# A graph and expert network on one core: where the two routers' logits are computed

## The reference, cut to what matters

```python
def _L0_ffn_ref(x, Wr, ...):            # x: layer norm of the sum, [6250, 256]
    rw = jax.nn.softmax(x @ Wr, axis=-1)            # Wr: [256, 8]
    topw, topi = jax.lax.top_k(rw, K)               # K = 2
    topw = topw / jnp.sum(topw, axis=-1, keepdims=True)
    ...
def _L1_ffn_ref(x, ..., gW, gb):
    gates = jax.nn.softmax(x @ gW + gb, axis=-1)    # gW: [256, 4], gb: [4]
    topv, topi = jax.lax.top_k(gates, TOPK)         # TOPK = 2
    topw = jax.nn.softmax(topv, axis=-1)
    ...
x = x + _L0_gnn_ref(_layernorm(x), ...)
x = x + _L0_ffn_ref(_layernorm(x), ...)
x = x + _L1_gnn_ref(_layernorm(x), ...)
x = x + _L1_ffn_ref(_layernorm(x), ...)
```

## Time and profile before

| | us |
|---|---|
| median of 3 runs | 6690.58 |
| lowest and highest | 6688.31, 6698.25 |
| the profiled execution's own time | 6698.42 |
| its span, first to last instruction | 6696.8 |
| TensorE busy | 4284.9 |
| VectorE busy | 3318.1 |
| GpSimd busy | 3481.7 |
| ScalarE busy | 827.6 |

### The profile page before, as it was taken

One profiled execution on the slowest core, in us unless ns is written; L12 is line 12 of the kernel. 1 busy time (PEld: TensorE's weight loads), 2 busy tenths in 40 slices (PEclk: granted clock), 3 DMA queues, 4 the chain that ended last, 5 costly groups with the idle time before them and its releaser, 6 DMA issues. The chain is left out here.

```text
span 6696.8 us, 90430 instructions
## 1 busy us (share of the span) xinstructions
PE 4284.9 (64%) x16771; PEld 3118.6 (47%) x16772; DVE 3318.1 (50%) x7834; ACT 827.6 (12%) x2019; POOL 3481.7 (52%) x3600
## 2 busy tenths in 40 slices
PE   1455566635666764556665379999971556667679
PEld 1333444423444443334443168888860344445435
DVE  6366666556566665656666521111126444444545
ACT  0200000020000002000000223322220000001322
POOL 3577777567777747777773060000016777774000
PEclk9777788867777887778887589999985778888789
DMA  5443333243333334333333241222225333333011
GB/s 184 126 111 106 106 106 106 71 140 106 106 106 106 106 90 121 106 106 106 106 106 89 77 132 38 64 64 51 65 67 152 105 105 105 105 105 97 1 46 44
DMA packets 485970, 642.49 MB, mean 96 GB/s; under 512 B 243204, under 2 KB 366208, under 8 KB 484096
## 3 DMA queue, kind: packets, MB, share of 16 engines
q0 software_dynamic: 175472, 478.82, 25.6%
q1 hardware_dynamic: 300880, 155.42, 8.3%
q10 hardware_dynamic: 9552, 7.61, 0.4%
HBM read 544.09 MB, written 97.86 MB: 96 GB/s over the span
## 5 line engine op out<-in xcount | busy, mean ns | idle before, releaser
L942 POOL DMA_INDIRECT rows<-table,ix x2352 | 2264.3, 963 | 741.5 <-issue 686.7
L1203 PE MATMUL acc<-rows,hot 128*128 x5856 | 1623.1, 435 | 227.2 <-DVE hot L1050 170.0
L1203 PEld LDWEIGHTS acc<-rows,hot 128*128 128x128 f32 x5856 | 1165.6, 212 | 640.9 <-issue 425.5
L1050 DVE TENSOR_TENSOR hot<-lanes,drel 128x256 f32<-128x256 f32 x1464 | 609.6, 422 | 580.0 <-PE acc L1203 577.3
L1249 POOL DMA_INDIRECT rows<-emb,ix x784 | 743.3, 948 | 261.2 <-issue 231.3
L1371 PE MATMUL acc<-rows,hot 128*128 x1952 | 571.1, 454 | 331.3 <-DVE hot L1292 312.3
L1044 DVE TENSOR_TENSOR rows<-rows,pw 128x1024 f32<-128x1024 f32 x588 | 711.2, 1210 | 0.0
L1371 PEld LDWEIGHTS acc<-rows,hot 128*128 128x128 f32 x1952 | 421.5, 228 | 463.7 <-issue 391.9
L1929 PE MATMUL p<-xt,w 128*128 128x256 f32 x2496 | 553.2, 380 | 26.1 <-DVE xt L1976 26.1
L1940 PE MATMUL p<-w,xT 128*128 128x256 f32 x2496 | 551.4, 379 | 0.0
L1929 PEld LDWEIGHTS p<-xt,w 128*128 128x128 f32 x2496 | 475.4, 190 | 91.0 <-issue 26.2
(11 more groups left out here) (394 smaller groups left out, 4166.2 us busy)
## 6 DMA issues: line engine op xcount, KB each, us to landing
rows<-table,ix POOLq DMA_INDIRECT x2352, 2.8
xg<-slots_in SPq DMA_DIRECT2D x632, 32.0 KB
slots_out<-ys SPq DMA_DIRECT2D x78, 256.0 KB
table<-hs SPq DMA_DIRECT2D x147, 130.0 KB, 2.0
own_row<-table SPq DMA_DIRECT2D x21, 896.0 KB, 11.3
slots_in<-zsp SPq DMA_DIRECT2D x9, 1664.0 KB, 22.2
xin<-in_x POOLq DMA_DIRECT2D x14, 896.0 KB, 5.6
rows<-emb,ix POOLq DMA_INDIRECT x784, 2.7
```

The lines of the kernel that those rows point to most:

```text
L942: pool.indirect_dma_start(rows[:, h * GB + k, 0:RW], None, table, bass.IndirectOffsetOnAxis(ap=ix[:, h, k:k + 1], axis=0)).then_inc(landed ...
L1050: v.tensor_tensor(hot[j][:, :, :], lanes[:, :, :].to_broadcast([P, 2, P]), c.drel[:, ds(q * W + j * 2, 2)].rearrange("p (k o) -> p k o", o ...
L1203: ins = nc.tensor.matmul(A, hot[j][:, k, :], four[:, j * 2 + k, :], start=False, stop=False, skip_group_check=True)
```

## The change

The routers no longer have a loop on TensorE and VectorE. `norm_stage` takes a pair (router weights, PSUM tile). With it, TensorE's list is written out for all 49 tiles: after the transposes of tile t come the two matmuls of tile t-1, which have the turned tile in `xT` as the stationary operand (128 x 128) and the router's weights (128 x E) as the moving one. Their result has the nodes on the partitions and goes to one PSUM tile `pG` of 49 x E columns, which fits in one bank and stays allocated until the router has read it. The router begins with one VectorE operation over all 49 tiles, a copy in router 1 and an addition of the bias in router 2; for this the bias is loaded onto all partitions. The load of `wr` moves ahead of norm 1. The semaphores of each router go from eight to three.

```diff
-def norm_stage(nc, kit, c, a, X, add, outs, want):
+def norm_stage(nc, kit, c, a, X, add, outs, want, route=None):
...
+                    if route is not None:
+                        wr, logits = route
+                        for t in range(NT + 1):
+                            if t < NT:
+                                pe.wait_ge(normed, t + 1)
+                                pe.wait_ge(kept, t // UT * UT + ring2(t % UT))
+                                for h in range(2):
+                                    ins = nc.tensor.transpose(pT[t % UT % 2][:, h, :],
+                                                              xs[:, t % UT, h * P:(h + 1) * P], c.ident[:, :])
+                                ins.then_inc(turned, 1)
+                            if t:
+                                m = t - 1
+                                pe.wait_ge(kept, UT + m + 1)
+                                for h in range(2):
+                                    nc.tensor.matmul(logits[:, m, :], outs["sbuf"][:, h, m * P:(m + 1) * P], wr[:, h, :],
+                                                     start=(h == 0), stop=(h == 1))
+                        return
...
-def router(nc, kit, c, xT, wr, E, gbias, at_f, w1, w2, gate):
+def router(nc, kit, c, pG, E, gbias, at_f, w1, w2, gate):
...
-        lt = sb("lt", [E, UT * P])
...
-        pL = [ps(f"pL{k}", [E, CH]) for k in range(2)]
-        pG = ps("pG", [P, UT, E])
-        prod, kept, turned, put, own = sem("prod"), sem("kept"), sem("turned"), sem("put"), sem("own")
-        asked, given, passed = sem("asked"), sem("given"), sem("passed")
+        own, asked, given = sem("own"), sem("asked"), sem("given")
         with nc.Block() as block:
-            @block.tensor
-            def _(pe):
-                with pe.Fori(0, NB) as i:
-                    pe.wait_ge(kept, i + 1)
-                    for m in range(2):
-                        for k in range(2):
-                            ins = nc.tensor.matmul(pL[m][:, :], wr[:, k, :], xT[:, k, ds(i * UT * P + m * CH, CH)],
-                                                   start=(k == 0), stop=(k == 1))
-                    ins.then_inc(prod, 1)
-                    pe.wait_ge(kept, i + 2)
-                    pe.wait_ge(put, i + 1)
-                    pe.sem_inc(passed, 1)
-                    for k in range(UT):
-                        ins = nc.tensor.transpose(pG[:, k, :], lt[:, k * P:(k + 1) * P], c.ident[0:E, 0:E])
-                    ins.then_inc(turned, 1)
...
-                for s in (kept, put, turned):
-                    dve.sem_inc(s, 1)
-                with dve.Fori(0, NB) as i:
-                    dve.wait_ge(prod, i + 1)
-                    dve.wait_ge(turned, i + 1)
-                    for m in range(2):
-                        to = lt[:, m * CH:(m + 1) * CH]
-                        if gbias is None:
-                            ins = v.tensor_copy(to, pL[m][:, :])
-                        else:
-                            ins = v.tensor_scalar(to, pL[m][:, :], gbias[:, :], None, ALU.add)
-                    ins.then_inc(kept, 1)
-                    dve.wait_ge(turned, i + 2)
-                    v.tensor_copy(logits[:, ds(i * UT, UT), 0:E], pG[:, :, :]).then_inc(put, 1)
                 ch = Chain(dve, own)
                 ch.n = 1
-                dve.wait_ge(put, NB + 1)
+                if gbias is None:
+                    ch.link(v.tensor_copy(logits[:, :, 0:E], pG[:, :, :]))
+                else:
+                    ch.link(v.tensor_tensor(logits[:, :, 0:E], pG[:, :, :], gbias[:, :, :].to_broadcast([P, NT, E]),
+                                            ALU.add))
...
-                    norm_stage(nc, kit, c, a, X, "input", {"sbuf": xT, "rows": slots_in, "rows_sb": rows}, "both")
                     loads(nc, kit, [(wr[:, :, :], a["L0_ffn_Wr"].rearrange("(k p) e -> p k e", p=P))])
-                    router(nc, kit, c, xT, wr, E0, None, pick, w1, w2, None)
+                    with kit.stage() as route:
+                        pG = route.ps("pG", [P, NT, E0])
+                        norm_stage(nc, kit, c, a, X, "input", {"sbuf": xT, "rows": slots_in, "rows_sb": rows}, "both",
+                                   (wr, pG))
+                        router(nc, kit, c, pG, E0, None, pick, w1, w2, None)
...
-                    (gb[:, :], a["L1_ffn_gb"])])
+                    (gb[:, 0, :], a["L1_ffn_gb"].rearrange("e o -> o e").to_broadcast([P, E1]))])
...
-                norm_stage(nc, kit, c, a, X, "scaled", {"sbuf": xT, "adds": rows, "scale": sumsq}, "turned")
-            with kit.stage() as st:
-                router(nc, kit, c, xT, gw, E1, gb, st.sb("pick", [P, NT, 2]), st.sb("w1", [P, NT, 1]),
-                       st.sb("w2", [P, NT, 1]), gate)
+                with kit.stage() as route:
+                    pG = route.ps("pG", [P, NT, E1])
+                    norm_stage(nc, kit, c, a, X, "scaled", {"sbuf": xT, "adds": rows, "scale": sumsq}, "turned",
+                               (gw, pG))
+                    router(nc, kit, c, pG, E1, gb, route.sb("pick", [P, NT, 2]), route.sb("w1", [P, NT, 1]),
+                           route.sb("w2", [P, NT, 1]), gate)
```

More of the change, by code:

```diff
@@ L2330, in program @@
             gate = rest.sb("gate", [P, NT, E1])
-            gw, gb = rest.sb("gw", [P, 2, E1]), rest.sb("gb", [E1, 1])
+            gw, gb = rest.sb("gw", [P, 2, E1]), rest.sb("gb", [P, 1, E1])
             with kit.stage() as st:
```

## The result

The changed kernel takes 6611.5 us (median of 4 runs, 6608.4 to 6615.5) against 6691.3 us for the kernel before: ratio 0.988, interval 0.9863 to 0.9897, 1.2% faster. The forecast was 6608 us. The profiled execution took 6608.4 us.

A forecast was written before the change was run, and what follows sets the result against it. No engine is full; serial stages bound it, the router loops being TensorE-VectorE chains. 90.5 - 5.6 - 2.9 + 0.8 = 82.8 us off 6698.42 gives 6615.6; median 7.8 lower, 6608 us; range 6598 to 6632.

The forecast's parts named there:

- router 1, memset to `max`: Router 1: 41.91 us shrink to 1.1, memset 0.39, PSUM copy 0.53 and waits some 0.1; 40.8 us saved.
- periods of full groups: Both norms: groups still follow each other at 11.01 and 10.12 us, the round of VectorE and ScalarE; cost 0.
- tail of norm 2: Last group of norm 2: 56 TensorE instructions, 12.3 us, end at 6344.3 instead of 6338.70; 5.6 us lost.
- tail of norm 1: Last group of norm 1: ScalarE's copy of the rows starts at 3805.0 instead of 3802.16, the last store 2.9 us later.
- load of `wr` moved: The `loads` stage goes ahead of norm 1, serial in either place: cost 0, bounds minus and plus 3.35 us.
- load of `gb`: The bias broadcast stands among loads that are broadcast already: cost 0, at most its own issue of 0.4 us.
- What bounds the kernel: Engines meet at each stage's end, so each us taken from or added to a stage moves the program's end as much.
- The price of a logit instruction: TensorE in the norms: 0.217 us per instruction, the weight load's spacing at any clock; four per tile, 0.87 us.
- The cover: Norms: TensorE's 9.1 us per group fit under periods of 10.12 and 11.01 us, so full groups cost nothing.
- the first rival: Norms: waits between transposes and logits leave holes, TensorE becomes the bound; 22 us more, 6630 us; chance 0.13.
- Loads that don't overlap: Norms: weight load and matmul run one behind the other, a tile takes 4.1 us; 6860 us; chance 0.03.
- Code fetching: TensorE's straight lists in the norms: a dozen more fetches at 1 to 3 us exposed, 6615 to 6640 us; chance 0.05.

The follow-up runs named there:

- the run with only the second half changed: Only norm 2, router 2 and the bias load changed against the kernel before: 6649.2 us, ratio 0.9935, 44.3 us less.
- The run with only the first half changed: Only norm 1 and router 1 changed against the kernel before: 6657.6 us, ratio 0.9947, 35.9 us less.
- The undisturbed burst: Changed kernel with all logits of each norm made in one burst behind its last transposes: 6683.8 us, ratio 0.9995 to the kernel before.
- the 64-column run: Changed kernel with two more matmuls per tile behind the logits, same stationary tile, 64 moving columns: 6661.3 us, ratio 0.9960 to the kernel before.

## Why the prediction was right

| step | predicted, us | measured in the profiles, us |
|---|---|---|
| router 1, memset to `max` | -40.8 | 41.91 to 1.02: -40.9 |
| router 2, memset to `max` | -49.7 | 50.60 to 0.82: -49.8 |
| fewer semaphores | -0.4 each | boundary behind router 1 from 1.38 to 1.03: -0.35 |
| periods of full groups | 0 | 11.00 and 10.12, unchanged |
| tail of norm 2 | +5.6 | first row of the stage to router 2's memset, 76.4 to 81.3: +4.8 |
| tail of norm 1 | +2.9 | first row to the landing of the last store: +2.5 |
| load of `wr` moved | 0 | ahead +2.4, behind -3.2: -0.8 |
| load of `gb` | 0, at most 0.4 | issue to the addition behind it, 3.64 to 4.34: +0.7 |
| sum | -82.8 | -84.0 |

(The measured sum takes the routers up to the next stage, 41.2 and 50.1.) The timed difference is 79.8 us, and its interval, 69 to 92 us, holds both sums. The profiled pair differs by 90.0 us; the 6 us beyond the table lie in stages that the change doesn't touch, nearly all ahead of norm 1, and the other profiles show that they move by chance.

That the forecast of 6608 us came within 4 us of the median is partly luck. Router 1's 40.8 us rest on one execution in which the old loop was slow; at the 38.27 us of the run with only the second half changed, the table's sum would be 80.4, next to the timed 79.8. That this is the typical value isn't shown: only these two profiles hold that loop. The run with only the first half changed fits it too: 35.9 us where 39.4 were expected. Small slips cancel or are too small to matter: 0.39 + 0.53 + 0.1 is 1.0 and not 1.1, and 3805.0 is 2.8 us and not 2.9 behind 3802.16.

**What bounds the kernel.** Right: the saving in each stage went through to the end unchanged. The stages between the routers took the same: from the first expert's weight load to the next weights' load 1246.7 us in both kernels.

**The price of a logit instruction.** Right as to clock and columns, a little high as a size. The undisturbed burst gives 0.213 us against the 0.217 read off and the earlier trace rows, and the 64-column run shows that the moving columns don't set it. That leaves the weight load or a fixed price per instruction. The old routers' small transposes, whose stationary operand has 8 rows instead of 128, speak against a fixed price: seven took 0.57 us together, less than 0.1 us apart. They are another kind of instruction, and no run changed the stationary operand alone. The Trainium skill ("TensorE: Matmul & The Clock Gate", section "LDWEIGHTS (loading the stationary operand)") gives a load the number of columns over 1.2 in ns, an estimate of 107 ns for 128 columns. That isn't what fp32 costs here: the measured 0.213 us is twice that. But a tile costs 1.17 us, not 1.30. Four logits instructions at 0.213 leave 0.32 for the two transposes, where a chain of transposes alone shows 0.43. The mix of transposes and logits is quicker than the two apart, which the prediction didn't count, and no run here says why. It explains norm 2's tail: 11.6 us from the last burst's release to the end instead of 12.3.

**The cover.** Right, and it is what the gain hangs on. Three runs show its edges: the same tile instead of the one before takes 65 us of the gain away, four more instructions per tile 52, all logits behind the norm 75 of 79, which leaves nothing that the times can tell. The holes of the first rival didn't come: in the steady stretch of the timeline transposes and logits follow each other without idle time. Besides the wait for the root, the one hole in a full group is the wait for tile 6's copy, 0.15 us on the side of the weight loads.

**The rivals.** Loads that don't overlap: refuted by the burst, 0.213 us apart though one instruction lasts 0.36 and its load 0.33. Code fetching: the second fetching queue went from 13 packets to 17, the first stayed at 53, and in the groups read on the timeline TensorE's idle time is all accounted for by ScalarE's copies and VectorE's `xs`. By the Trainium skill's rule ("Runtime: NRT & Kernel Launch", section "Instruction fetch mechanics") straight code is fetched ahead; the traces agree in so far as the lists cost nothing that shows. What a fetch that is waited for would cost, 1 to 3 us in the prediction, no run shows.

**Smaller steps off.** The `loads` stage isn't neutral in its place: ahead of norm 1 it costs 2.4 us between the attention layers and the norm, while 3.2 went from behind it. The broadcast of `gb` costs 0.7, not 0.4 at most. The issue itself grew only from 0.42 to 0.47 us; the rest comes between it and the addition.

## What to carry to other kernels

Here a product with a 128x128 stationary operand cost 0.21 us per instruction whether 4, 8 or 64 columns moved, and 196 of them took as long as router 1's old loop, so turning the product round made it hardly cheaper; look for the orientation in which it needs no partner and can be laid under a stage where the engine idles. It is free only while all of the engine's work in a period fits the period, and only if each piece depends on something done a step ago: the same instructions one tile earlier cost 65 us here. What remains is the tail of the last period, so look at what the engine still owes when that begins; and when an order on ScalarE is rewritten as a loop, look in the profile for table loads that the new loop brought in.

## What the runs showed of the hardware that was not expected

- **The clock didn't rise for a TensorE that was never idle.** In the burst behind norm 1 the engine was busy 41.98 of 42.10 us, weight loads 41.89, and the granted clock stayed at 0.50 (1.2 GHz) all the while; so it did in both routed norms of the changed kernel, busy 79% and 85%. The old router loops, with 448 moving columns per instruction and idle a quarter of the time, were granted 0.87 and 0.74. So the busy time of the profile alone doesn't tell the granted clock. For the logits the clock made no difference: the instructions of the earlier trace rows, at 1.00, are (5.29 - 0.36)/23 = 0.214 us apart on the timeline of the kernel before (the 0.217 there came from rounded starts):

```profile
112.33 5.29 PE L843 MATMUL pa<-avec,wt 128*128 128x8 f32 x24 [16.65 <-DVE wt L805]
```

- **The old loop's time was partly the clock's.** A round's eight matmul instructions with 448 moving columns took 3.17 us or 4.87, and router 1's unchanged loop 38.27 us in one profile and 41.91 in another, at mean granted clocks of 0.95 and 0.87.
- **A table load came with a loop's shape.** With the root first in the loop of norm 1, 1.28 us in each of seven groups, six of them on the path; with the first root outside the loop, one load in all. Norm 2, with the same code, had none in either form; why the two differ no run shows.
- **A 16-byte row broadcast to 128 partitions** held its stage 0.5 to 0.9 us longer than the same four values on four partitions: from its issue to the addition behind it 4.2 to 4.6 us in the ten profiles that have it, 3.6 and 3.7 in the two that don't.
